# Feed-forward stages of a transformer chain: the next batch's transposes queued ahead of the present batch's output

## The reference

```
h = layer_norm(x) * g + be                  # 512 x 320
proj = h @ w1 + b1                          # 512 x 2560
a, gate = split(proj, 2)                    # 512 x 1280 each
x = (a * gelu(gate)) @ w2 + b2 + x          # 512 x 320
```

## Time and profile before

| | us |
|---|---|
| median of three runs | 4240.84 (4230.23 to 4243.2) |
| profiled execution, its own time | 4228.71 |
| its span | 4226.6 |
| PE matmul busy | 3774.3 (89%) |
| DVE busy | 1754.6 (42%) |
| ACT busy | 1538.5 (36%) |
| POOL busy | 677.8 (16%) |
| feed-forward stage s2, about | 1932 to 2232 of the span |
| feed-forward stage s5, about | 3102 to 3403 of the span |

### The profile page before, as it was taken

The page is one execution under the profiler, slowest core; times in us unless marked ns, Lnnn a source line. Parts: engine busy times, 40 slices in busy tenths (PEclk is TensorE's granted clock), DMA queues, the critical chain, the costliest instruction groups (busy, mean ns, idle before and its releaser), DMA issues.

```text
span 4226.6 us, 39174 instructions
## 1 busy us (share of the span) xinstructions
PE 3774.3 (89%) x15784; PEld 1553.7 (37%) x15784; DVE 1754.6 (42%) x2338; ACT 1538.5 (36%) x2113; POOL 677.8 (16%) x438
## 2 busy tenths in 40 slices
PE   8999899998989899998996898999889978868997
PEld 3333333333333333334442333333334455542332
DVE  2524335252534435352123665666611222225553
ACT  3424243342524344341111554555521111114553
POOL 1414223141423324240000000000000000000000
PEclk9999999999979989999996999999999976758998
DMA  2000000001000000001000000000010010000000
GB/s 80 16 15 23 12 23 4 27 12 46 16 14 22 11 19 7 26 10 49 0 1 19 1 1 16 4 12 1 1 49 0 0 31 8 4 23 4 5 1 25
DMA packets 43235, 67.35 MB, mean 16 GB/s; under 512 B 5296, under 2 KB 30320, under 8 KB 43056
## 3 DMA queue, kind: packets, MB, share of 16 engines
q1 hardware_dynamic: 43056, 64.85, 5.1%
HBM read 62.22 MB, written 2.62 MB: 15 GB/s over the span
## 4 chain that ended last, share of the span: by engine, by line
PE 79%; DVE 11%; ACT 3%; issue 3%; DMA 2%; SPq 1%; POOL 0%; DVEq 0%; ACTq 0%; POOLq 0%
PE bank L498 11%; PE bank L576 7%; PE bank L431 7%; PE bank L465 6%; PE bank L922 5%; PE bank L551 5%; DVE heads L879 4%; PE bank L864 4%; PE bank L1411 4%; PE bank L847 4%; PE bank L1413 3%; PE bank L1039 3%; DVE negm L528 3%; PE bank L520 2%; PE bank L975 2%
## 5 line engine op out<-in xcount | busy, mean ns | idle before, releaser
L879 DVE TENSOR_REDUCE heads<-bank 128x2 f32<-128x1024 f32 x480 | 587.8, 1225 | 513.9 <-PE bank L864 511.6
L528 DVE TENSOR_REDUCE negm<-bank 128x2 f32<-128x1024 f32 x320 | 387.9, 1212 | 954.5 <-PE bank L520 954.5
L431 PE MATMUL bank<-weights,mixed 128*128 128x320 f32 (+1 forms) x1376 | 398.0, 448 | 19.8 <-DVE mixed L1440 12.6
L551 PE MATMUL bank<-weights 64*128 64x512 f32 x1280 | 411.7, 628 | 0.0
L498 PE MATMUL bank<-hT,heads 128*128 128x512 f32 x720 | 382.6, 653 | 16.1 <-issue 8.9
L431 PEld LDWEIGHTS bank<-weights,mixed 128*128 128x128 f32 (+1 forms) x1376 | 261.7, 194 | 160.1 <-issue 32.8
L610 DVE RECIPROCAL rec<-ox 128x128 f32<-128x128 f32 x320 | 279.0, 918 | 94.2 <-ACT ox L615 88.5
L847 PE MATMUL bank<-heads 32*128 32x512 f32 x1920 | 312.2, 634 | 5.9 <-ACT weights L892 3.0
L892 ACT ACTIVATE weights<-bank 128x1024 f32<-128x1024 f32 x238 | 230.6, 1021 | 104.7 <-PE bank L847 104.5
L864 PE MATMUL bank<-heads 32*128 32x512 bf16 x960 | 194.0, 401 | 65.8 <-DVE heads L879 57.2
L587 POOL TENSOR_TENSOR heads<-probs 128x1024 f32<-128x1024 f32 x40 | 95.8, 2394 | 838.0 <-ACT probs L566 838.0
(11 more groups left out here) (172 smaller groups left out, 5162.6 us busy)
## 6 DMA issues: line engine op xcount, KB each, us to landing
heads<-in_wqk SPq DMA_DIRECT2D x40, 384.0 KB, 3.0
heads<-in_wqk SPq DMA_DIRECT2D x40, 320.0 KB, 2.9
ctx_in<-in_ctx SPq DMA_DIRECT2D x16, 384.0 KB, 3.5
weights<-in_L_xattn_wo SPq DMA_DIRECT2D x2, 1600.0 KB, 13.8
x_res<-in_x SPq DMA_DIRECT2D x4, 640.0 KB, 12.8
out<-x_res SPq DMA_DIRECT2D x1, 2560.0 KB, 8.7
weights<-in_L_xattn_w_ff SPq DMA_DIRECT2D x1, 1600.0 KB, 13.0
weights<-in_L_xattn_ff_w SPq DMA_DIRECT2D x1, 1600.0 KB, 12.0
```

The lines of the kernel that those rows point to most:

```text
L431: last = nc.tensor.matmul(M.SM[t % 2][:, 0:D], v["OT"][0:w, c, t * P:t * P + P], v["wo"][0:w, c, :], start=c == 0, stop=c == nch - 1)
L528: nc.vector.tensor_reduce(M.negm[:, u % 2, i, 0:2], M.ROWS[:, :, :], AX.X, ALU.max, negate=True).then_inc(s.sem("max"), 1)
L551: nc.tensor.matmul(out[:, g, :], v["KT"][strip, u % 3, i * P:i * P + P], v["QT"][strip, u % 3, :], start=True, stop=False)
L879: nc.vector.tensor_reduce(v["negm"][:, tile, qb, 64 * half:64 * half + 64].rearrange("p (g k) -> p g k", g=2)[:, :, at], M.ROWS4[:, :, :], ...
```

## The change

In `inputs_pe` of a feed-forward stage the first two groups of transposes of every batch but the first wait for the multiplies of tiles 8 and 9 of the batch before, whose banks they overwrite. In `ff_pe` the transposes of batch b + 1 are issued between the last tile of batch b and its output; the start wait of a batch stands ahead of its output; the first batch's transposes stand behind the stage's start wait. ACT no longer waits for the last residual addition in batches after the first: it waits for the last first-layer products of the batch before (they read the `hT` that it overwrites), and for the multiplies also at j = 0 and 1. DVE does the norm of the next batch behind the multiply of tile 4, after a wait for the batch's own three groups of transposes.

```diff
@@ inputs_pe
                 if k >= 2:
                     hold(pe, s.sem("in_evac" + s.tag), after(b - s.first, n_in(s), k - 1))
+                elif s.kind == "ff" and b > s.first:
+                    pe.wait_ge(s.sem("ot"), after(b - 1, NF, NF - 1 + k))
                 for t in range(TB):
@@ ff_pe
+            start(pe, s, s.first)
+            inputs_pe(pe, s, s.first)
+            pe.wait_ge(s.w_in, 16 * s.n_loads)
             for b in range(s.first, s.first + B):
-                inputs_pe(pe, s, b)
-                start(pe, s, b)
-                pe.wait_ge(s.w_in, 16 * s.n_loads)
                 hold(pe, s.sem("in_evac" + s.tag), after(b - s.first, 3, 3))
...
+                if b + 1 < s.first + B:
+                    inputs_pe(pe, s, b + 1)
                 if b == s.first:
                     ff_weights(pe, s, "wo_in")
+                start(pe, s, b)
                 out_pe(pe, s, b)
@@ ff_act
+                if b == s.first:
+                    start(act, s, b)
+                else:
+                    act.wait_ge(s.sem("a_ps"), after(b, NF, 0))
                 inputs_act(act, s, b)
-                start(act, s, b)
                 for j in range(NF):
                     act.wait_ge(s.sem("g_ps"), after(b, NF, j + 1))
-                    if j >= 2:
+                    if j >= 2 or b > s.first:
                         act.wait_ge(s.sem("ot"), after(b, NF, j - 1))
@@ ff_dve
                                                    in1=v["gate"][:, j % 2, :], op0=ALU.add, op1=ALU.mult).then_inc(s.sem("ot"), 1)
-                norm_next_dve(dve, s, b)
+                    if j == 4:
+                        dve.wait_ge(s.sem("in_ps" + s.tag), after(b - s.first, n_in(s), n_in(s)))
+                        norm_next_dve(dve, s, b)
                 out_dve(dve, s, b)
```

## The result

The changed kernel took 4200.95 us (median of 19 runs, 4176.04 to 4230.61) where the kernel before took 4224.98 (19 runs, 4207.72 to 4243.2): ratio 0.9944, 95% interval 0.9924 to 0.9964. The profiled execution has a span of 4193.9 us, 32.7 less than before.

What follows compares the result with a forecast made beforehand. TensorE (PE), busy 89% of the span, was taken as the bound. Six seams at 1.88 us gave 11.3 us, other terms nothing; 4235.7 - 11.3 = 4224.4 us, range 4212 to 4238.

Steps and rivals of the forecast that it cites:

- Six seams: Stretches between one batch's output and the next first layer, three per feed-forward stage; each 2.92 us was to go.
- group 0: First four transposes of the next batch; 0.52 us, free inside the old hole, covered by tile 9's GELU and multiply.
- groups 1 and 2: Next two groups of transposes, ahead of the output; 0.52 us each on the path, starting the output 1.04 later.
- stall at tile 7: PE's wait for tile 5's multiply behind the moved norm; predicted not to hold PE, margin 1.2 us.
- two items costed at nothing: The norm's move into the middle of the tiles, and ACT's changed waits in later batches; each predicted to cost nothing.
- the gain per seam: Seam of 2.92 us removed, less 1.04 us of transposes now ahead of the output: 1.88 us, six times, 11.3.
- The hole: PE's standstill between a batch's first layer and its output, waiting for tile 9's GELU and multiply; taken as 1.65 us.
- upper bound of 12.1: Most the six seams could give: 2.92 less two groups at 0.45, 2.02 us each, in all 12.1 us.
- The mean of the four is 4235.7: Starting time from four known executions of the kernel before; 4235.7 less 11.3 gave the forecast 4224.4 us.
- Rival 1: Granted clock of later stages falls otherwise after the time shift: from 16.3 us less to 15.1 more; chance 0.2.
- Rival 2: Transposes at the seams not hidden, group 0 held by its wait, group 2 by ACT: gain only 3.2 us; chance 0.1.
- rival 3: Moved norm holds PE before tile 7, 8 times; at 11 us of norm, 21.5 us slower overall; chance 0.05.

Runs made afterwards that it cites:

- Experiment 9: Changed kernel with the first group of transposes waiting for the multiply of tile 9 instead of tile 8; one execution, batches 72.1 us against 70.9.
- experiment 5: Changed kernel with the next batch's norm back behind tile 9, transposes still ahead of the output; ratio 1.0108 against the kernel before.
- experiment 3: Kernel before with only the norm moved behind tile 4; ratio 0.9992 against the kernel before.
- experiment 10: Changed kernel with ACT's old wait for the last residual addition put back behind its evacuations; one execution, 4185.57 us, batches 70.9.
- experiment 2: Changed kernel timed again with no edit; ratio 0.9957 against the kernel before, 12 runs.
- experiment 7: Changed kernel timed a third time with no edit; ratio 0.9985 against the kernel before, 12 runs.
- experiment 6: Changed kernel with eight more DVE statistics ahead of the norm in the middle of the tiles; ratio 1.004 against the kernel before.
- experiment 8: Kernel before with only the output's wait for tile 9's multiply moved to before its tenth product; ratio 0.9977 against the kernel before.

## Why the prediction was right or wrong

- **What the change does, right.** Six seams closed; group 0 free, groups 1 and 2 on the path for 1.09 us together (I had 1.04); no stall at tile 7; margin 1.26 us (I had 1.2). Experiment 9 shows that the cover of group 0 counts, and experiment 5 that without the norm's move the early transposes cost 38.8 us. Experiments 3 and 10 confirm two items costed at nothing.
- **The term that was mis-sized: the gain per seam, "2.92 - 1.04 = 1.88 us".** It measured 2.33 (73.22 to 70.89). I had taken output and first layer at their old durations, but something else now runs directly ahead of each. At the second seam of s2 the output took 21.80 us behind the hole and 21.54 behind the transposes, and the first four products of the first layer 1.96 behind the seam's last wait and 1.72 behind the output: 2.92 - 1.09 + 0.26 + 0.24 = 2.33. The hole did not shrink; my 1.65 is that of the first seam, and at the second it is 1.55 in both kernels. Six seams make 14.0 us, and the first batches of the two stages, which vary, take 0.2 back: 13.8 us instead of 11.3, outside the upper bound of 12.1 that I had given. My bound let transposes vary and not the work that follows them.
- **The step that failed: "The mean of the four is 4235.7".** I placed the forecast on four executions. 113 of them have a mean of 4221.7, and the 19 of the comparison a median of 4224.98. That is 10.7 us too high at the start, of the 23.4 by which 4224.4 missed 4200.95; the mis-sized term is 2.5; the remaining 10.2 is luck, the scatter of that comparison: experiments 2 and 7 gave smaller gains with the same kernel, and by the pool it is 8 to 10.
- **The range** took the four executions' extremes as the scatter of the kernel. An execution scatters by 12 us, from 4187 to 4245. An estimate from what is now known: 4221.7 - 13.8 = 4207.9, already below my range of 4212 to 4238, give or take some 7 us for a median of 19 executions that scatter by 12; 4200.95 lies at the edge of that.
- **Rival 1, right as a mechanism but misplaced.** The granted clock decides the scatter, and not only in the gated stage: s6 took 346.1 to 363.8 us over the traces, and s1, ahead of everything that was changed, 928.8 to 955.4. It acts from run to run of one kernel. I treated it as what the shift in time would do; it needs no shift. One batch of s1 took 242.1 us in one trace of the kernel before and 227.3 in the other. That fits what the Trainium skill (TensorE: Matmul & The Clock Gate, What's actually happening) says of windows that run freely of the kernel; the traces show the level of the clock and not the windows.
- **Rival 2** (transposes exposed) did not happen; **rival 3** was costed too low by its own arithmetic, 1 us for each us of stall: experiment 6 gives 1.9 us of stall and 1.9 to 3.6 us on the batch.
- **Left open:** what decides the level of the clock. Batch one of s2 took 81.4 us in two traces of the changed kernel and 82.4 in experiments 7 and 10; over the first 25 us of the stage the granted clock was 0.86 in the first two and 0.80 in the others. Why it falls one way or the other, no run shows.

## What to carry to other kernels

Where independent work stands behind a dependent wait on the engine that bounds the kernel, put it in front, but move what it needs at least as far: the transposes alone would have made this kernel slower by 0.9% to 1.1%. Look at each wait for how much of the following work really needs it: the output needed the last tile only for the last product of each block, and saying so gave 12.7 us against the 13.8 of the whole reordering. And before a time is forecast to within 0.3%, know the scatter of the kernel before: compare stage by stage in the traces, where a feed-forward stage repeats to about 1 us, and its later batches to a few hundredths, while the whole moves by ten.

## What the runs showed of the hardware

- What ran directly ahead of a group of products changed its time, at a granted clock of 1.00 all along. The output took 21.77 and 21.80 us behind a standstill of PE, 21.73 directly behind the first layer (experiment 8) and 21.54 directly behind transposes. The first four products of a tile took 1.95 and 1.96 behind a standstill of 0.96 us, 1.91 directly behind the tile before, and 1.72 directly behind the output. So against work on all 128 rows ahead a standstill cost 0.23 to 0.26 us beyond its own length, and against the end of a first-layer tile, whose last products have 64 rows each, only 0.04 to 0.07. Most of it is overlap: in the timeline the first layer starts at 2067.76, while the chain counts it from the end of the output at 2067.93, 0.17 us later, and behind a standstill there is nothing to overlap. That it is the 64 rows which leave less of this was not tested.
- A stall can pull the clock down behind it. The holes of 1.55 and 1.65 us did so in none of the eight batches of the kernel before (one of them in the earlier trace rows). A stall of 1.87 us in the middle of tiles was followed by a clock of 0.57 to 0.62 over 4 us in four of eight places (experiment 6). In experiment 9, with two waits of PE around its transposes, the clock fell at the first seam of s2 and stayed at 1.00 at the second:

```profile
1983.60:1987.90 4.30, 2.21 (x13) 2.00 (x14) 0.75 (x1) 2.12 (x3) 0.00 (x0) 0.84 0.00 0
1987.90:1992.00 4.10, 4.10 (x12) 2.73 (x12) 0.00 (x0) 0.78 (x1) 0.00 (x0) 0.75 0.00 0
2057.10:2061.00 3.90, 1.77 (x15) 1.45 (x14) 0.75 (x1) 2.10 (x3) 0.00 (x0) 1.00 0.00 0
```

- The low level can last far longer than the wait ahead of it, with PE busy nearly throughout: 31.29 of 32 us at 0.51 behind a DMA wait of 3.61 us.
